# The accumulator's base x + xn moved from GpSimd's additions to ScalarE activations, and GpSimd's scatter DMAs issued without additions between them

## The reference

```
xn = layernorm(x)
x = x + attention(xn) + ffn(xn)
ffn(xn) = xn + expert_out
```

## Time and profile before

| | us |
|---|---|
| median of 3 runs | 321.93 |
| lowest and highest run | 321.22 and 323.74 |
| span of the profiled execution, first to last instruction | 314.8 |
| early attention ends on TensorE | about 162 |
| first and last result rows sent by GpSimd | 169.2 and 292.0 |

### The profile page before, as it was taken

How to read it: one execution, slowest core, us unless ns; L and a number is a source line. 1 busy time by engine, 2 the same in 40 slices (tenths; PEclk the granted TensorE clock), 3 DMA queues, 4 the chain that set the end, 5 groups by cost and what they waited for, 6 DMA issues and landing times.

```text
span 314.8 us, 6507 instructions
## 1 busy us (share of the span) xinstructions
PE 273.9 (87%) x2030; PEld 256.8 (82%) x2030; DVE 222.7 (71%) x523; ACT 160.1 (51%) x365; POOL 233.2 (74%) x357
## 2 busy tenths in 40 slices
PE   4998878899999999999699999999999999986200
PEld 4797767689999999998689999999999999986100
DVE  5856999858888888887666777777777774850155
ACT  3574663134444444446246777777777775431000
POOL 6799713688888888888603788888898888888440
PEclk9797998579999999999699999999999999988555
DMA  7976000371111111111142788888878841111498
GB/s 234 337 248 227 1 3 0 103 276 47 49 47 50 46 56 52 47 49 47 47 115 85 234 245 256 252 250 252 253 260 243 267 133 44 42 52 51 148 356 314
DMA packets 27469, 45.77 MB, mean 145 GB/s; under 512 B 5328, under 2 KB 16208, under 8 KB 27440
## 3 DMA queue, kind: packets, MB, share of 16 engines
q1 hardware_dynamic: 21312, 33.86, 34.2%
q0 software_dynamic: 4544, 9.84, 8.9%
q10 hardware_dynamic: 1584, 1.73, 1.5%
HBM read 27.73 MB, written 17.68 MB: 144 GB/s over the span
## 4 chain that ended last, share of the span: by engine, by line
PE 67%; DVE 13%; POOL 8%; DMA 4%; issue 4%; ACT 2%; SPq 1%; ACTq 0%; DVEq 0%; POOLq 0%
PE bank L820 11%; PE bank L667 8%; POOL rows_y L568 7%; PE bank L808 6%; PE bank L691 6%; PE bank L810 6%; PE bank L809 6%; PE bank L681 4%; PE bank L643 4%; PE bank L645 3%; PE bank L644 3%; PE bank L793 3%; PE bank L616 2%; DVE acc L324 2%; DMA router_sb<-router_wT_dram 2%
## 5 line engine op out<-in xcount | busy, mean ns | idle before, releaser
L568 POOL DMA_INDIRECT rows_y<-xn,row_i x78 | 81.0, 1038 | 29.2 <-ACT xn L994 15.7
L896 ACT ACTIVATE feat<-z_sb 128x512 f32<-128x512 f32 x64 | 39.9, 631 | 64.7 <-DVE z_sb L1089 64.4
L541 POOL DMA_INDIRECT slots_x<-xn,slot_i x64 | 63.8, 997 | 10.9 <-issue 10.9
L1082 DVE TENSOR_REDUCE neg_max<-bank 128x16 f32<-128x512 f32 x64 | 42.7, 683 | 19.0 <-PE bank L645 18.9
L808 PE MATMUL bank<-xT_high,w_high 128*128 128x256 f32 x156 | 47.3, 303 | 1.0 <-DVE xT_low L1284 0.5
L810 PE MATMUL bank<-xT_high,w_low 128*128 128x256 f32 x156 | 44.0, 282 | 0.0
L809 PE MATMUL bank<-xT_low,w_high 128*128 128x256 f32 x156 | 43.9, 282 | 0.0
L1089 DVE TENSOR_TENSOR z_sb<-bank,neg_max 128x512 f32<-128x512 f32 x64 | 42.5, 681 | 0.5
L820 PE MATMUL bank<-w_tile,hidden 128*128 128x128 f32 x312 | 41.0, 275 | 0.0
L667 PEld LDWEIGHTS bank<-v_aug,feat 128*128 128x128 f32 x256 | 33.6, 212 | 8.3 <-issue 6.9
L667 PE MATMUL bank<-v_aug,feat 128*128 128x36 f32 x256 | 34.0, 293 | 5.3 <-DVE att L1114 5.3
(11 more groups left out here) (152 smaller groups left out, 550.0 us busy)
## 6 DMA issues: line engine op xcount, KB each, us to landing
w_tile<-w_expert_dram SPq DMA_DIRECT2D x39, 384.0 KB, 3.6
slots_x<-w_tile SPq DMA_DIRECT2D x39, 144.0 KB, 2.2
x_tile<-slots_x SPq DMA_DIRECT2D x39, 144.0 KB
acc<-x_dram SPq DMA_DIRECT2D x8, 256.0 KB, 5.7
xn<-rows_y SPq DMA_DIRECT2D x8, 256.0 KB, 6.4
w_tile<-rows_y SPq DMA_DIRECT2D x8, 256.0 KB, 6.5
out_dram<-acc ACTq DMA_DIRECT2D x5, 256.0 KB, 4.3
rows_y<-xn,row_i POOLq DMA_INDIRECT x78, 3.0
```

Of the source, the lines that this page charges most:

```text
L541: pool.indirect_dma_start(slots_x, bass.IndirectOffsetOnAxis(slot_i[k][:, i:i + 1], 0), xn[:, j, :], None).then_inc(scattered[n % FLIGHT], 16)
L568: pool.indirect_dma_start(rows_y, bass.IndirectOffsetOnAxis(row_i[:, k, t:t + 1], 0), y_tile(k, t), None)\
L896: act.activation(feat[par][n][:, :], z_sb[n][:, :], ACT.Exp).then_inc(feat_ready, 1)
L1082: dve.tensor_reduce(neg_max[n][:, :], args(n), AX_X, ALU.max, negate=True).then_inc(z_negmax, 1)
```

## The change

GpSimd's `add_xn` is removed. In its place VectorE computes `base_scale` = rstd + 1 once, 128x32, and ScalarE replaces each tile of `acc` by x (rstd + 1) + shift, which is x + xn, with one Identity activation (`set_base`), 32 in all. In step b of the early attention, from 1 to 12, `set_base` does tiles 3b-3 and 3b-2 ahead of `feat_0` and tile 3b-1 ahead of `feat_3`, as far as there are tiles: three in each of steps 1 to 10, two in step 11, none in step 12. `base_added` counts 32 whole tiles in place of 64 halves, and the waits for it are adapted: `add_projection(b)` waits for 2b + 2.

```diff
@@ tiles and semaphores @@
+        base_scale = sb("base_scale", [P, NT])
+        base_scaled = sem("base_scaled")
@@ gpsimd @@
-            def add_xn(n):
-
-                j, cols = half_tile(n)
-                pool.tensor_tensor(acc[:, j, cols], acc[:, j, cols], xn[:, j, cols], ALU.add).then_inc(base_added, 1)
...
                     if n >= FLIGHT:
                         pool.wait_ge(scattered[n % FLIGHT], 16 * (n // FLIGHT))
-                    add_xn(n)
                     pool.indirect_dma_start(slots_x, bass.IndirectOffsetOnAxis(slot_i[k][:, i:i + 1], 0),
                                             xn[:, j, :], None).then_inc(scattered[n % FLIGHT], 16)
...
-            pool.wait_ge(base_added, 2 * NT)
+            pool.wait_ge(base_added, NT)
@@ scalar @@
+            def set_base(first, end):
+
+                if first == 0:
+                    act.wait_ge(base_scaled, 1)
+                    act.wait_ge(xn_by_pool, NG)
+                    act.wait_ge(xn_by_act, NG)
+                for j in range(first, min(end, NT)):
+                    act.activation(acc[:, j, :], acc[:, j, :], ACT.Identity, bias=shift[:, j:j + 1],
+                                   scale=base_scale[:, j:j + 1]).then_inc(base_added, 1)
...
                 links(0)
+                if 1 <= b < EARLY:
+                    set_base(3 * b - 3, 3 * b - 1)
                 if front:
                     features(0, f, f_par)
...
+                if 1 <= b < EARLY:
+                    set_base(3 * b - 1, 3 * b)
                 if front:
                     features(3, f, f_par)
...
-            act.wait_ge(base_added, 2 * NT)
+            act.wait_ge(base_added, NT)
@@ vector @@
+            dve.wait_ge(rstd_done, NG)
+            dve.tensor_scalar(base_scale[:, :], rstd[:, :], 1.0, None, ALU.add).then_inc(base_scaled, 1)
             for n in range(2):
                 dve.wait_ge(w_feat_copied, n + 1)
...
-                dve.wait_ge(base_added, 4 * b + 4)
+                dve.wait_ge(base_added, min(2 * b + 2, NT))
```

## The result

| | median us | lowest and highest of 5 runs | ratio to before, 95% interval |
|---|---|---|---|
| before | 321.93 | 320.85, 323.74 | |
| after | 396.21 | 395.81, 402.52 | 1.2349 [1.2281, 1.2418] |

The forecast was 321.8 us. The page of the changed kernel, against the earlier trace rows: TensorE's busy time has grown by 17.3 us, the span by 81.6 us, and the strips (40 slices of 9.9 us) show TensorE all but idle from slice 11 to 15, about 99 to 149 us.

A forecast was written before the change was run, and what follows sets the result against it. TensorE's own work was taken to set the pace until 162 us, the scatter ending beside it. 314.8 + 0 + 0 + 0 - 0.12 = 314.7 us of span; 7.1 outside it gives 321.8, range 320.2 to 323.6.

The forecast's parts named there:

- The DMAs move up, steps of 1.29, last start 140.3, SP's loads near 143.: GpSimd's scatter: steps fall from 1.51 to 1.29 us, last start from 154.70 to 140.3, SP's loads from 157 to 143.
- ScalarE's 32 activations are hidden.: ScalarE, early attention: 15.4 us of new activations fit into idle time ahead of `feat_3` and `feat_0`; cost 0.
- -0.12 us by the second `w_low`.: VectorE at step 12: the second `w_low` falls from 805 to 679 ns without GpSimd beside it; -0.12 us.
- GpSimd's wait ahead of its first send near 28 us, L793 with nothing ahead at 162.: GpSimd's wait grows from 13.50 to some 28 us; TensorE's first transpose of sorted rows stays at 162.0 without idle time.
- This term is 0 us, though 14 us vanish from GpSimd.: End of GpSimd's scatter: nobody waited for SP's loads, so ending it sooner only lengthens GpSimd's idle time; 0 us.
- the slower ones: Rivals: activations stick out ahead of ScalarE's `feat_0`, 326.6 us, chance 0.04; one more TensorE clock fall, 325.1 us, 0.03.
- The pair of sends in the earlier trace: Two indirect GpSimd DMAs in a row among the result sends, starts 1.29 us apart, taken as the scatter's new step.
- The median lies 7.1 us above the span (start and end of the program outside it).: Whole program: 321.93 us median against 314.8 span; the same distance was added to the forecast span.
- The granted clock between 148 and 162 about 0.75.: TensorE after its 2.54 us pause: the granted clock stays at 0.75, partly at the lower level.

The follow-up runs named there:

- e17: The changed kernel itself, measured once more on chip 0: 315.11 us against 316.36 before, ratio 0.9969.
- e11: The kernel before with 14 more TensorE semaphore increments, which nobody reads, in each of steps 1 to 12; chip 9: 346.68 us against 348.34.
- e4: The kernel before with each addition of xn behind its scatter DMA in place of ahead of it; chip 1: 323.57 us against 319.43.
- e2: The changed kernel with an unread 128x64 GpSimd addition ahead of each scatter DMA; chip 1: 326.97 us against 319.43 before.
- e15: The changed kernel with an unread GpSimd addition of the old size ahead of each scatter DMA, on chip 4: 327.62 us against 320.94 before.
- e3: The changed kernel with a GpSimd memset of 128x1 ahead of each scatter DMA; chip 1: 394.07 us against 319.43 before.

## Why the prediction was wrong

- *The DMAs move up, steps of 1.29, last start 140.3, SP's loads near 143.* Right: 1.26, 138.06, and the loads at 140.42.
- *ScalarE's 32 activations are hidden.* Right: 479 ns, steps of 7.84 with ScalarE busy for 4.98. ScalarE's waits for `z_sb` fell from 64.4 us to 53.1 in e17, by 11.3 where 15 were forecast, which changes nothing. e17 puts the price of the whole change at -0.3% [-0.7, +0.1] where nothing stalls.
- *-0.12 us by the second `w_low`.* Right in the rows: the three `w_low` take 1.90 us in place of 2.02, and the pause is 2.42 in e17 and in the changed kernel's own profile for 2.54 before. It is too small for the times to show. (The 679 ns of the third `w_low` are in the trace, not in the earlier trace rows, which has the first two.)
- *GpSimd's wait ahead of its first send near 28 us, L793 with nothing ahead at 162.* True in e17 (29.79 and 162.16), false in the changed kernel's first profile (102.08 and 234.04).
- ***"This term is 0 us, though 14 us vanish from GpSimd."* This step failed.** It asked only who waits for the DMAs to end. It took the 0.52 us of other work and idle time between two DMAs for time that can be taken out at no cost, when on chips 1, 9 and 10, and in the runs of the result, that time was what kept TensorE's increments flowing. What the term measured in its place is 71.9 us, the delay of L789. None of the rivals had that mechanism: the slower ones looked at ScalarE and at the clock, with 4.8 and 3.3 us as their prices. The pair of sends in the earlier trace rows was used for its duration and not asked what TensorE does beside it.
- *"The median lies 7.1 us above the span (start and end of the program outside it)."* Failed too, and it was the one visible warning. Start and end are about 1.8 us by the other profiles; the other 5.3 are most likely waits that this profile didn't contain. The timed runs of before thus spent time in a way that its profile couldn't explain, and I gave it a harmless name.
- *The granted clock between 148 and 162 about 0.75.* Right: 0.75 in e17, and 0.75 in the same stretch of the changed kernel's own profile (220 to 233.7 us). Over 50 to 162 us, with the gaps, it was 0.59, so partly at the lower level, where e17 has 0.89: it fell after TensorE had stood. It is a consequence of the stall.

The Trainium skill, "SBUF — State Buffer", Who interferes with whom, gives DMA ports of its own and says that "PE and ACT never wait on anyone". That is about data ports. TensorE did wait here, 52.99 us at the longest, with the same DMA share (0.21) as in e17 without the stall; what came late were signals, of which that rule doesn't speak. The Trainium skill, "VectorE: DVE Perf Modes", section on the TRN2 errata, advises to space dense completion increments that come from several engines. e11 is the nearest test: 14 more increments a step, of TensorE alone, show no harm (346.68 against 348.34 us). What spacing helped here is that of indirect DMAs.

What is shown: on chips 1, 9 and 10 indirect DMAs of GpSimd at steps of 1.195 to 1.385 us stall TensorE. At 1.51 they delay its first transpose of sorted rows by 0.2 and 2.4 us on chip 1 (162.36 in e4, 164.53 in e2) and by 2.4 on chip 4 (164.58 in e15). At 2.54 (chip 10) the attention isn't delayed at all. On chip 9 the loss is 42.3 us at 1.46 and still 15.8 at 1.51. Plain DMAs at 0.7 do no harm on chip 4. On chips 0 and 6, 1.26 does nothing. What stays open: the path on which the increments are held, and whether only TensorE's are; whether the chip makes the difference or the session in which it was used; whether the mean density decides, each single gap, or how many DMAs are in flight (a landing takes 2.3 us, so about two are at 1.26 a step); and whether plain DMAs would do it on a chip that was seen to stall in its scatter. No variant beat the kernel before by more than its interval on any chip.

## What to carry to other kernels

The time that an engine leaves between its DMAs can be what keeps other engines' signals moving: before packing indirect DMAs closer, see what TensorE does beside the densest stretch that the kernel already has. Here half a microsecond between them was nearly enough on chip 1, and not on chip 9. Account for the difference between the profiled span and the timed median; if it is larger than in other kernels of the kind, the profile and the times may come from different conditions. And a change at such an edge must be timed on more than one chip, since chip 0 gave 0.997 and the runs of the result 1.235.

## What the runs showed of the hardware that I had not expected

- TensorE's semaphore increments reached their readers 4.7 to 54.5 us late, in order, while increments of ScalarE and VectorE took 0.05 to 0.14 us in the two places looked at. In e3 GpSimd stood 4.18 us ahead of an instruction that waits for nothing of TensorE.
- How much is lost depends steeply on the step: 74.1 us at 1.26, 42.3 at 1.46 and 15.8 at 1.51 on chip 9.
- An indirect DMA of GpSimd takes 0.96 us with 128 rows of 576 bytes, the same with rows of 64 bytes, and 0.89 with 64 rows; a plain one takes 0.54. Ahead of one that directly follows another stand 0.30 us, and a 0.12 us memset disappears in them (step 1.27).
- Chips (each in its one session) differ by far more than runs do: the kernel before took 315.25 to 348.34 us in the medians of six chips, and the changed one 315.11 on chip 0 and 396.21 in the runs of the result.
